# Graph attention with peaked softmax: order of turned chunks, first maxima and first piece maxima in the strip loop

## The reference

```python
def _L0_gnn_ref(x, mask, W, a_src, a_tgt):
    proj = jnp.einsum('nf,hfo->hno', x, W)                       # N 8192, F 128, O 128, H 4
    s_src = jnp.einsum('hno,ho->hn', proj, a_src)
    s_tgt = jnp.einsum('hno,ho->hn', proj, a_tgt)
    scores = jax.nn.leaky_relu(s_src[:, :, None] + s_tgt[:, None, :], negative_slope=0.2)
    attn = jax.nn.softmax(mask[None, :, :] + scores, axis=1)
    vals = jnp.einsum('hij,hjo->hio', attn, proj)
    vals = jax.nn.elu(vals + x[None, :, :])
    return vals.mean(axis=0)
h = jnp.maximum(_layernorm(x, axis=-1), 0.0)
return x + _L0_gnn_ref(h, adj, W, a_src, a_tgt)
```

## Time and profile before

| | |
|---|---|
| median of three runs | 926.92 us |
| the profiled execution | 926.4 us, span 924.6 us |
| TensorE busy / mean granted clock | 713.4 us (77%) / 0.933 |
| VectorE busy | 788.5 us (85%) |
| ScalarE busy | 696.0 us (75%) |
| GpSimd busy | 286.9 us (31%) |
| HBM read and written | 281.80 MB and 12.65 MB, 318 GB/s over the span |

### The profile page before, as it was taken

The page is one execution under the profiler, slowest core; times in us unless marked ns, Lnnn a source line. Parts: engine busy times, 40 slices in busy tenths (PEclk is TensorE's granted clock), DMA queues, the critical chain, the costliest instruction groups (busy, mean ns, idle before and its releaser), DMA issues.

```text
span 924.6 us, 14987 instructions
## 1 busy us (share of the span) xinstructions
PE 713.4 (77%) x5007; PEld 577.6 (62%) x5007; DVE 788.5 (85%) x790; ACT 696.0 (75%) x1187; POOL 286.9 (31%) x164
## 2 busy tenths in 40 slices
PE   1507687988978888988988887987988987769883
PEld 1506476777766766776766766766776766644431
DVE  3886789989999999989999999999989996535885
ACT  0498667977977977967977977977976977746883
POOL 1000202242132242231342242242242232125885
PEclk8657979999999999999999999999999999988997
DMA  9999999999999999999999999999999997927222
GB/s 246 329 374 394 373 350 372 351 359 371 350 368 371 372 371 371 365 349 370 373 371 370 372 371 371 371 371 371 371 371 372 358 274 207 253 41 189 58 58 58
DMA packets 224101, 294.93 MB, mean 319 GB/s; under 512 B 4545, under 2 KB 218049, under 8 KB 224065
## 3 DMA queue, kind: packets, MB, share of 16 engines
q1 hardware_dynamic: 214848, 290.27, 91.7%
q0 software_dynamic: 9216, 4.20, 3.8%
HBM read 281.80 MB, written 12.65 MB: 318 GB/s over the span
## 4 chain that ended last, share of the span: by engine, by line
PE 40%; issue 16%; ACT 14%; DVE 11%; DMA 8%; POOL 5%; SPq 4%; ACTq 0%; POOLq 0%; DVEq 0%
PE ps L450 31%; ACT ps L534 13%; PE ps L418 7%; DMA arena<-in_adj 5%; DVE arena L622 5%; POOL arena L404 4%; DMA sums<-arena 3%; DVE ps L627 3%; SPq L347 3%; DVE arena L605 1%; PE ps L437 1%; SPq L332 1%; POOL arena L408 1%; PE ps L425 1%; DVE arena L626 1%
## 5 line engine op out<-in xcount | busy, mean ns | idle before, releaser
L534 ACT ACTIVATE ps<-ps,arena 128x1024 f32<-128x1024 f32 x512 | 555.9, 1086 | 180.7 <-DVE arena L626 111.0
L450 PE MATMUL ps<-ident,arena 128*128 128x128 f32 x4096 | 559.8, 284 | 75.9 <-ACT ps L534 57.8
L450 PEld LDWEIGHTS ps<-ident,arena 128*128 128x128 f32 x4096 | 463.0, 145 | 162.2 <-ACT ps L534 138.8
L605 DVE TENSOR_TENSOR arena<-arena 128x3072 f32<-128x3072 f32 (+2 forms) x115 | 359.3, 3125 | 13.8 <-DMA arena<-in_adj 10.6
L391 POOL DMA_INDIRECT sums<-arena x64 | 175.3, 2738 | 530.1 <-DVE arena L661 230.8
L418 PE MATMUL ps<-ident,arena 128*128 128x128 f32 x512 | 75.0, 295 | 104.5 <-DVE ps L627 61.8
L418 PEld LDWEIGHTS ps<-ident,arena 128*128 128x128 f32 x512 | 62.4, 152 | 111.4 <-issue 67.2
L622 DVE TENSOR_REDUCE arena<-ps 128x1 f32<-128x1024 f32 x64 | 78.3, 1224 | 44.4 <-PE ps L418 42.7
L534 ACT ACTIVATION_READ_ACCUMULATOR ps<-ps,arena 128x1 f32 x512 | 100.4, 196 | 0.0
L601 DVE TENSOR_TENSOR arena<-arena 128x3072 f32<-128x3072 f32 (+2 forms) x23 | 71.8, 3123 | 14.6 <-DMA arena<-in_adj 14.6
L627 DVE SCALAR_TENSOR_TENSOR ps<-ps,arena 128x1024 f32<-128x1024 f32 x64 | 82.1, 1282 | 0.3 <-issue 0.3
(11 more groups left out here) (76 smaller groups left out, 202.3 us busy)
## 6 DMA issues: line engine op xcount, KB each, us to landing
arena<-in_adj SPq DMA_DIRECT2D x160, 1536.0 KB, 14.9
arena<-in_adj SPq DMA_DIRECT2D x16, 512.0 KB, 7.1
arena<-in_adj SPq DMA_DIRECT2D x8, 1024.0 KB, 11.1
sums<-arena SPq DMA_DIRECT2D x1, 4160.0 KB, 22.3
arena<-sums SPq DMA_DIRECT2D x8, 512.0 KB, 7.2
out<-arena SPq DMA_DIRECT2D x16, 256.0 KB, 2.3
sums<-arena POOLq DMA_INDIRECT x64, 8.4
w_sb<-in_L_gnn_W SPq DMA_DIRECT2D x1, 256.0 KB, 2.7
```

What stands on the lines that cost most here:

```text
L450: mm = pe.transpose(turned_ps[n % 2][:, m, :], piece(i, r, nq)[:, m, q * P:(q + 1) * P], ident[:, :])
L534: act.activation(turned_ps[n % 2], turned_ps[n % 2], ACT.Exp, scale=KAPPA, bias=cert[:, i, q, G:G + 1], accum_out=cert[:, i, q, r:r + 1]). ...
L605: dve.tensor_tensor(acc_of(nq), acc_of(nq), piece(i, r, nq), ALU.max).then_inc(f_acc, 1)
```

## The change

The order of chunks in a wide strip gets its sixth and seventh exchanged, so that (0,2) comes before (2,1). `EARLY` becomes 0, so that a strip's first maxima are turned before any of its chunks. The maximum of pieces 0 and 1 is split, from strip 2 on: its first set is taken by a new `first_set_max` between `find_rows` and the third column maximum of the strip before, the other two sets stay in `piece_max`. The maximum with piece 2 moves ahead of `find_same`.

```diff
+    FRONT = [(0, 0), (1, 0), (2, 0), (0, 1), (1, 1), (0, 2), (2, 1), (1, 2), (2, 2)]
...
+    def split(g, i):
+
+        return subs(g, i) == NQ and (not known(g) or number(g, i) >= 2)
...
+        if nq == NQ:
+            return FRONT + [(r, q) for r in range(LEAD, G) for q in range(nq)]
         return [(r, q) for q in range(nq) for r in range(LEAD)] + [(r, q) for r in range(LEAD, G) for q in range(nq)]
...
-    EARLY = 2
+    EARLY = 0
...
                 if r == 1:
+                    cols = slice(P if split(g, i) else 0, nq * P)
                     dve.wait_ge(f_in[slot(i, 0)], landed(g, i, 0))
                     dve.wait_ge(f_in[slot(i, 1)], landed(g, i, 1))
-                    dve.tensor_tensor(acc_of(nq), piece(i, 0, nq), piece(i, 1, nq), ALU.max).then_inc(f_acc, 1)
+                    dve.tensor_tensor(acc_of(nq)[:, :, cols], piece(i, 0, nq)[:, :, cols], piece(i, 1, nq)[:, :, cols],
+                                      ALU.max).then_inc(f_acc, 1)
                 else:
                     dve.wait_ge(f_in[slot(i, r)], landed(g, i, r))
+                    if r == 2 and split(g, i):
+                        dve.wait_ge(f_acc0, Q - 1)
...
+            def first_set_max(g, i):
+
+                nq = subs(g, i)
+                dve.wait_ge(f_in[slot(i, 0)], landed(g, i, 0))
+                dve.wait_ge(f_in[slot(i, 1)], landed(g, i, 1))
+                dve.tensor_tensor(acc_of(nq)[:, :, 0:P], piece(i, 0, nq)[:, :, 0:P], piece(i, 1, nq)[:, :, 0:P],
+                                  ALU.max).then_inc(f_acc0, 1)
...
                     if q == nq - 1 and not first_strip(g, i):
                         find_rows(*before)
+                    if q == nq - 1 and not last_strip(g, i) and split(*after):
+                        first_set_max(*after)
                     column_max(g, i, q)
...
                     piece_max(*after, 1)
+                if not last_strip(g, i) and nq == NQ:
+                    piece_max(*after, 2)
                 if not first_strip(g, i):
                     find_same(*before)
-                if not last_strip(g, i):
+                if not last_strip(g, i) and nq < NQ:
                     piece_max(*after, 2)
```

More of the change, by code:

```diff
@@ L207, in peaked_path @@
     f_acc = sem("pieces_max")
+    f_acc0 = sem("first_set_of_two_pieces_max")
     f_max = sem("substrip_max")
```

## The result

| | before | after |
|---|---|---|
| median of the runs | 926.46 us (922.95 to 927.3, 4 runs) | 913.63 us (912.74 to 914.72, 4 runs) |
| the profiled execution's span | 924.6 us | 912.6 us |

The ratio is 0.9869, with a 95% interval of 0.984 to 0.9898. The direction was right. The size was not, and neither was the step that carried most of the forecast, the exchange of two chunks.

A forecast was written before the change was run, and what follows sets the result against it. The stream of `adj` was taken to pace the wide strips. Exchange -4.8, split -1.0 and boundary to strip 21 -1.5 sum to -7.3 us, from 926.9 to 919.6 us; range 915.8 to 924.5.

The forecast's parts named there:

- the exchange of two chunks: Wide strips: piece 4's load goes out one chunk earlier, 1.1 us, so the stream hardly runs short: -4.8 us.
- What bounds the kernel: Wide strips: the stream of `adj` paces them at 34.5 us and 371 GB/s; the engines need 34.2 us.
- unchanged dry stretches: Rival, 10%: the stream's slow spells (153 to 226 GB/s) have another cause than piece 4's late issue and stay; 924.4 us.
- strips of 33.5 us: Rival, 4%: the engines, not the stream, bound the wide strips, which shrink to VectorE's 33.5 us; 907.0 us.
- strip 1's stall: Rival, 6%: in strip 1 the added wait of 6.7 us is not covered by ScalarE's idle; 926.3 us.
- L624 waiting in each strip: Rival, 5%: the first-set maximum waits for piece 1 of the next strip in every strip; 949 us.
- 5.8 us in all: Stream of `adj`: the loss against 371 GB/s, summed over six stretches of 1.5 to 2.5 us.
- line between two leads: Piece 4's lead of 2.9 us, placed between 1.8 and 3.1, still loses 0.17 us, over six strips 1.0 us.
- The split: VectorE's strip takes 33.5 us in place of 34.2, so it catches up at strip 20: -1.0 us.
- The boundary to strip 21: Without two early chunks the first exponential comes 2.2 us earlier, less 0.7 for strip 20's late sixth: -1.5 us.
- Strip 21's clock: TensorE may stay at its higher clock with the idle gone; about 1.5 us possible for strip 21, counted as 0.
- strip 1, `find_same` and strip 0: Strip 1's added wait is covered, `find_same` ends 2.7 us later before its reader, strip 0's turning is hidden: nothing.

The follow-up runs named there:

- The filling: The kernel before, with eight matmuls that nobody reads put behind each strip's first maxima, where TensorE idles 2.92 us: 916.28 us, ratio 0.9894.

## Why the prediction was right in direction and wrong in size and in its main step

**What bounds the kernel** was right: the stream of `adj` paces the wide strips at 34.4 us, and its losses were the time to be had. The rivals with unchanged dry stretches, with strips of 33.5 us, with strip 1's stall and with L624 waiting in each strip all fell, each by the row that the prediction had named. The first of them was right in its doubt that the order of the chunks makes the dry stretches, though not in what would follow from it. That the stream is the bound is firmer now: VectorE has 0.87 us to spare and the strips are no shorter. The Trainium skill (DMA: Bandwidth & Descriptors, "Where 436 GB/s comes from") takes about 358 GB/s as what binds loads from HBM. The 12.6 MB of a wide strip would need 35.1 us by it, an estimate from the page's figure. The strips take 34.4, which is 366 GB/s for the loads alone, and the measurement decides.

**The step that failed is the exchange, "-4.8 us",** and with it the sentence before it, that the dry stretches come of piece 4's late issue by the order of the chunks. The late issue is real, but what made it late in some strips and not in others was the clock. The prediction had the row for it (0.95 of full in the slower strips) and set it aside with "how much of the dry stretches that explains I can't separate". The separation was in the trace: each dry stretch has a fall of the clock ahead of it. The experiments put the exchange at nothing in the changed kernel (913.8 without it), and at 20.3 us *lost* without the removal of the early chunks, which the forecast costed at nothing. It called their removal free and the exchange the gain; it is the other way round.

**The size of the loss, "5.8 us in all",** was too small. It counted what six windows of 1.5 to 2.5 us had lost. Counted by strips, each from one last landing to the next, the kernel before is slow in seven strips, of which these are four (strips 3, 5, 6 and 19; of the excess of strip 6 about 1 us is in the changed kernel too):

```profile
114.58:150.31 35.73, 29.45 (x209) 25.53 (x209) 31.46 (x28) 26.55 (x46) 2.69 (x3) 0.85 1.03 358
...
186.02:221.51 35.49, 30.19 (x227) 25.96 (x225) 32.85 (x29) 28.43 (x52) 11.65 (x5) 0.95 1.06 363
221.51:257.54 36.03, 30.43 (x227) 26.12 (x228) 32.59 (x29) 28.34 (x51) 8.50 (x5) 0.95 1.05 358
...
671.37:707.25 35.88, 30.70 (x233) 26.53 (x231) 32.96 (x29) 28.50 (x51) 12.75 (x5) 0.95 1.08 371
```

Strips 3 to 20 took 742.28 - 114.58 = 627.7 us before and 734.95 - 114.66 = 620.3 after, so 7.4 us were to be had. The last row had no dry stretch to be counted at all, and moves 371 GB/s. Taking a further 1.0 us off by a line between two leads made it 4.8: of the missing 2.5 us, 1.5 are the count and 1.0 the line. The lead of piece 4 itself came out at 494.7 + 16.4 - 505.6 = 5.5 us by the issues of pieces 3 and 4 in the strip that begins to load at 483 us, where the forecast had 2.9. The issues of L355, with the greatest time to landing of the first two:

```profile
L355 SPq DMA_DIRECT2D arena<-in_adj x2: 3854/4086/4317, 490.6 to 494.7; - x2
...
DMA to landing us min/median/max: 16.4/16.4/16.4
...
L355 SPq DMA_DIRECT2D arena<-in_adj x1: 542/542/542, 505.6 to 505.6; - x1
```

**Why the removal of the early chunks brings it.** The engines' strip gets shorter than the stream. In the kernel before, engines at 34.2 and a stream at 34.4 leave 0.2 us per strip to catch up with, and a fall costs VectorE about 1 us: its last maxima at 361.1 and 396.3, with the fall at 368 between them, lie 35.2 us apart. By this estimate the engines need five strips to be in time again, and a fall within these is paid. With the forecast's 33.1 us for ScalarE and 33.5 for VectorE there is about 1 us per strip. The forecast had both numbers and called them free; they are the cover without which a fall is paid. The removal alone does not keep the clock up: with `EARLY = 0` alone it fell ten times, before it eight times up to the end of the stream. The falls are gone in the trace of the whole change, where TensorE's gaps are 1.18 us ahead of the second maxima and mostly 1.2 to 1.8 us ahead of the first (2.2 to 2.6 with `EARLY = 0` alone), and that is worth the last 2 us at most. The filling shows the other way to the same gain: no falls to be covered, without any cover.

**The split, "-1.0":** at strip 20 the maximum now starts with the landing (734.97 against 734.95), where it was 1.06 us late. As forecast, in that trace. In the times the split adds nothing that can be measured to the other two parts; alone it gives 0.6%.

**The boundary to strip 21, "-1.5":** 10.2 - 8.4 = 1.8 us, and the idle ahead of it 1.19 where "about 2" was forecast. The sixth exponential of strip 20 waits 1.12 us, and starts 8.05 us behind the first where it was 7.48: 0.6 us later for 0.7 costed.

**Strip 21's clock, "it could give about 1.5 us; I take 0":** from the first exponential of strip 21 to the scatter 1.7 us are gained, 1.2 of them by the third exponential, and the fall at 784 is gone. Where the cause of an idle gap goes, the clock that falls behind it should be counted as the likely case and not as an end of the range.

**At nothing, and nothing it was:** strip 1, `find_same` and strip 0. L445, which reads what `find_same` writes, starts at 515.70 in the strip of 498, 17.6 us after the first exponential. Before it was 521.34 - 504.60 = 16.7 us: 0.9 us later at no cost.

In all, -7.3 (stream), -1.0, -1.8 and -1.7 are 11.9 of the 12.0 us between the spans.

## What to carry to other kernels

When a stream paces a kernel and some of its stages are longer, lay the granted clock beside the stages before you explain them by the order of the loads, and count the loss over the whole stream, not by the dips. An engine that is "only" as fast as the stream is no cover: each of its delays is paid until it has caught up at the difference of the two, so making it 1 us faster per stage was worth most of the stream's gain here, though it is never the bound. And a part of a change may be harmful alone and harmless in company; the exchange here is both, which only runs of the parts could tell.

## What the runs showed of the hardware

- TensorE's clock fell behind an idle gap of 2.93 us between two groups of eight matmuls, but not in every strip that has this gap: the kernel before has it in each wide strip and nine falls up to 790 us, mostly in successive strips, and none between 406 and 678 us. Eight small matmuls in the gap (1.92 us) kept the clock up from 120 to 809 us; with `EARLY = 0`, where gaps of 2.2 to 2.6 us stand ahead of the first maxima, they did not (six falls).
- With a gap of 1.18 us there and 2.2 to 2.6 us ahead of the first maxima (`EARLY = 0` alone) it still fell ten times. With 1.18 and mostly 1.2 to 1.8 us (the changed kernel) it did not in the trace between 97 and 795 us, and once, at 254 us, in the version with the old order in strip 20.
- One fall makes a group of eight transposes take 1.94 us in place of 1.06. The same fall costs a strip nothing, 0.2 to 0.9 or 1.5 us, by which group it meets and what time the engines have to spare.
